# A fused Mamba and feed-forward kernel: the order of loads, activations and exponents inside a tile

## The reference, cut to what matters

```python
proj = einsum('bsd,ed->bse', layernorm(x), in_proj_w)     # gate | hBC | dt
hBC = silu(causal_conv(hBC, conv_w, 4 taps) + conv_b)     # hs | B | C
dt = clip(softplus(dt + dt_bias), 0, 100)
L = exp(segsum(dt * A))                                   # decays within a chunk of 128
Y = diagonal part (C B^T * L) @ (hs*dt) + carried part + hs*D
g = Y * silu(gate);  g = rmsnorm over each group(g) * norm_w
x = x + g @ out_proj_w.T
x = x + ffn(layernorm(x))                                 # 512 -> 1792 -> 512, quantised activations
```

## Time and profile before

| | us |
|---|---|
| median of 3 runs | 1877.3 (1875.56 to 1877.73) |
| the profiled execution, its own time | 1877.94 |
| span of the profiled execution | 1876.1 |
| TensorE busy | 1750.3 (93%) |
| VectorE busy | 1263.9 (67%) |
| GpSimd busy | 1184.9 (63%) |
| ScalarE busy | 840.9 (45%) |
| mean granted TensorE clock | 0.992 of full speed |

### The profile page before, as it was taken

The page is one execution under the profiler, slowest core; times in us unless marked ns, Lnnn a source line. Parts: engine busy times, 40 slices in busy tenths (PEclk is TensorE's granted clock), DMA queues, the critical chain, the costliest instruction groups (busy, mean ns, idle before and its releaser), DMA issues. The chain is left out here.

```text
span 1876.1 us, 34372 instructions
## 1 busy us (share of the span) xinstructions
PE 1750.3 (93%) x10392; PEld 1407.7 (75%) x10392; DVE 1263.9 (67%) x1892; ACT 840.9 (45%) x1273; POOL 1184.9 (63%) x873
## 2 busy tenths in 40 slices
PE   6899999999999999999999989999999998999998
PEld 5677787778777877787778777787778776788886
DVE  7777647772787287736874677557854774977776
ACT  4555345543564355535653555345634553322221
POOL 3487658865777568846775588558765777632430
PEclk9899999999999999999999999999999998999999
DMA  2322102210222022202230222012210221111101
GB/s 95 92 64 85 41 29 80 85 46 22 68 80 68 0 79 85 74 0 73 69 94 3 57 80 84 19 51 67 81 40 29 80 75 42 46 57 34 45 23 45
DMA packets 71341, 107.23 MB, mean 57 GB/s; under 512 B 16740, under 2 KB 25060, under 8 KB 71304
## 3 DMA queue, kind: packets, MB, share of 16 engines
q1 hardware_dynamic: 70296, 105.38, 18.8%
q10 hardware_dynamic: 1008, 1.38, 0.2%
HBM read 103.51 MB, written 3.15 MB: 57 GB/s over the span
## 5 line engine op out<-in xcount | busy, mean ns | idle before, releaser
L794 PE MATMUL proj<-xhi,w_hi 128*128 128x512 f32 x1080 | 447.2, 414 | 80.8 <-DVE gate L1116 76.9
L796 PE MATMUL proj<-xhi,w_lo 128*128 128x512 f32 x1080 | 423.7, 392 | 0.0
L795 PE MATMUL proj<-xlo,w_hi 128*128 128x512 f32 x1080 | 423.6, 392 | 0.0
L794 PEld LDWEIGHTS proj<-xhi,w_hi 128*128 128x128 f32 x1080 | 203.1, 188 | 174.7 <-DVE gate L1116 101.7
L1097 DVE SCALAR_TENSOR_TENSOR v<-proj,par_sb,v 128x510 f32<-128x510 f32 x378 | 279.9, 742 | 72.5 <-ACT v L590 51.7
L492 POOL TENSOR_TENSOR g_lo<-gated,g_hi 128x512 fp32r<-128x512 f32 x128 | 164.0, 1284 | 198.4 <-ACT g_hi L723 198.3
L427 POOL TENSOR_TENSOR w_lo<-w_raw,w_hi 128x512 fp32r<-128x512 f32 x144 | 182.5, 1286 | 138.0 <-ACT w_hi L568 138.0
L796 PEld LDWEIGHTS proj<-xhi,w_lo 128*128 128x128 f32 x1080 | 203.3, 188 | 45.0
L795 PEld LDWEIGHTS proj<-xlo,w_hi 128*128 128x128 f32 x1080 | 203.8, 189 | 35.7
L467 POOL TENSOR_TENSOR gated<-hs,gate 128x512 f32 (+1 forms) x128 | 190.0, 1506 | 51.0 <-DVE hs L1222 51.0
L590 ACT ACTIVATE v<-proj,par_sb 128x512 f32<-128x512 f32 x126 | 97.8, 776 | 248.4 <-PE proj L796 248.4
(11 more groups left out here) (164 smaller groups left out, 3360.4 us busy)
## 6 DMA issues: line engine op xcount, KB each, us to landing
w_raw<-in_win SPq DMA_DIRECT2D x144, 256.0 KB, 4.2
fade_l<-faded SPq DMA_DIRECT2D x128, 256.0 KB, 3.7
wo_raw<-in_wout SPq DMA_DIRECT2D x64, 256.0 KB, 2.6
M<-in_w SPq DMA_DIRECT2D x14, 512.0 KB, 3.8
row_r<-rows SPq DMA_DIRECT2D x256, 3.0 KB
row_l<-rows SPq DMA_DIRECT2D x256, 3.0 KB
cb<-in_w SPq DMA_DIRECT2D x7, 512.0 KB, 3.3
out<-resid SPq DMA_DIRECT2D x8, 256.0 KB, 2.0
```

The costliest lines, as they stand in the source:

```text
L794: e.matmul(o, hi_l, hi_r, start=first, stop=False)
L795: e.matmul(o, hi_l, lo_r, start=False, stop=False)
L796: return e.matmul(o, lo_l, hi_r, start=False, stop=last)
```

## The change

Four reorderings, with no instruction added or removed. SyncE issues the weight pair first in a step, ahead of wo_raw, rows and fade. ScalarE scales wo_raw between the weight casts and the second tap, casts it to wo_hi behind that tap, and does the gate's first tanh ahead of the first exponential. TensorE does the next tile's exponents ahead of y. VectorE does the gate's first silu ahead of the first weighing (so both weighings now stand between the gate's two silus), and hs's first silu behind the second step of the second convolution, no longer behind the first.

```diff
--- before.py
+++ after.py
@@ -333,6 +333,8 @@
             load_rows(0, 0)
 
             def step(g, j, par_, nxt, nxt2, ahead):
+                if nxt2:
+                    load_pair(9 * g + j + 3, split.at(g, j, 0))
                 sp.wait_ge(wolo.sem, wolo.at(g, j, 0))
                 sp.dma_start(wo_raw[:, :], wout[TPG * g + j, :, :]).then_inc(woraw.sem, 16)
                 if nxt:
@@ -340,8 +342,6 @@
                     load_rows(TPG * g + j + 1, 1 - par_)
                     sp.wait_ge(pdone.sem, pdone.at(g, j, 1))
                     load_fade(TPG * g + j + 1)
-                if nxt2:
-                    load_pair(9 * g + j + 3, split.at(g, j, 0))
 
             def window(g, nxt):
                 if nxt:
@@ -680,28 +680,29 @@
                 if nxt2:
                     act.wait_ge(ready.sem, ready.at(g, j, 0))
                     upper_pair(par_, 9 * g + j + 3)
-                if nxt:
-                    tap3(1, w, ready.at(g, j, 2), silu.at(g, j, 0))
-                    act.wait_ge(gdone.sem, gdone.at(g, j, 0))
-                    hs_tanh(hs[:, 1 - par_, :], 0, taken.at(g, j, 1))
                 act.wait_ge(woraw.sem, woraw.at(g, j, 16))
                 act.wait_ge(gused.sem, gused.at(g, 0, 0))
                 e.activation(wo_raw[:, :], wo_raw[:, :], ACT.Copy,
                              scale=par_sb[:, bass.ds(TPG * g + j, 1), K + 2:K + 3].rearrange("p a b -> p (a b)"))\
                     .then_inc(woscaled.sem, 1)
+                if nxt:
+                    tap3(1, w, ready.at(g, j, 2), silu.at(g, j, 0))
                 act.wait_ge(woscaled.sem, woscaled.at(g, j, 1))
                 e.copy(wo_hi[:, bass.ds(j, 1), :].rearrange("p a f -> p (a f)"), wo_raw[:, :])\
                     .then_inc(wohi.sem, 1)
+                if nxt:
+                    act.wait_ge(gdone.sem, gdone.at(g, j, 0))
+                    hs_tanh(hs[:, 1 - par_, :], 0, taken.at(g, j, 1))
                 if ahead:
                     bounded(g, j + 1, 0)
                 if nxt:
                     hs_tanh(hs[:, 1 - par_, :], 1, taken.at(g, j, 2))
                 if ahead:
                     bounded(g, j + 1, 1)
-                    exponential(g, j + 1, 0)
                 if nxt:
                     gate_tanh(gate[:, 1 - par_, :], 0, ready.at(g, j, 3))
                 if ahead:
+                    exponential(g, j + 1, 0)
                     exponential(g, j + 1, 1)
                 if nxt:
                     gate_tanh(gate[:, 1 - par_, :], 1, ready.at(g, j, 4))
@@ -939,9 +940,9 @@
                 turn()
                 if nxt:
                     unit(1)
-                y()
                 if ahead:
                     exponents(g, j + 1, 1 - par_)
+                y()
                 if nxt:
                     unit(2)
                     unit(3)
@@ -1087,7 +1088,7 @@
             e.tensor_scalar(par_sb[:, :, 0:K + 1], par_sb[:, :, 0:K + 1], 0.5, None, ALU.mult).then_inc(s_halved, 1)
             e.tensor_scalar(parbc_sb[:, :, :, :], parbc_sb[:, :, :, :], 0.5, None, ALU.mult).then_inc(s_halved, 1)
 
-            def conv_rest(h, weights, ntap, nconv, between=(), banks=proj):
+            def conv_rest(h, weights, ntap, nconv, between=None, banks=proj):
 
                 dve.wait_ge(tap.sem, ntap)
                 dst, src = per_batch(v[:, h, :]), per_batch(banks[h][:, :])
@@ -1097,8 +1098,8 @@
                     e.scalar_tensor_tensor(dst[:, :, d:S], src[:, :, 0:S - d], weights(K - 1 - d),
                                            dst[:, :, d:S], ALU.mult, ALU.add)\
                         .then_inc(taken.sem if d == K - 1 else convs.sem, 1)
-                    if d <= len(between):
-                        between[d - 1]()
+                    if d == 2 and between:
+                        between()
 
             def tile_weights(t):
                 return lambda k: par_sb[:, bass.ds(t, 1), k:k + 1].rearrange("p a b -> p (a b)")
@@ -1214,7 +1215,7 @@
                 if nxt:
                     conv_rest(0, w, tap.at(g, j, 1), convs.at(g, j, 0))
                     conv_rest(1, w, tap.at(g, j, 2), convs.at(g, j, 2),
-                              (lambda: hs_silu(hs[:, 1 - par_, :], 0, tanh.at(g, j, 1)),))
+                              lambda: hs_silu(hs[:, 1 - par_, :], 0, tanh.at(g, j, 1)))
                 own = tile_weights(t)
                 for h in range(2):
 
@@ -1223,11 +1224,9 @@
                                            ALU.mult, ALU.add).then_inc(ysum.sem, 1)
                 if nxt:
                     hs_silu(hs[:, 1 - par_, :], 1, tanh.at(g, j, 2))
+                    gate_silu(gate[:, 1 - par_, :], 0, tanh.at(g, j, 3))
                 if ahead:
                     weigh_own(g, j + 1, 0)
-                if nxt:
-                    gate_silu(gate[:, 1 - par_, :], 0, tanh.at(g, j, 3))
-                if ahead:
                     weigh_own(g, j + 1, 1)
                 if nxt:
                     gate_silu(gate[:, 1 - par_, :], 1, tanh.at(g, j, 4))
```

## The result

The changed kernel takes 1774.0 us (median of 4 runs, 1773.8 to 1775.0) against 1876.7 for the kernel before in the same comparison: a ratio of 0.9454, 95% interval 0.9438 to 0.9470. The profiled execution's own time is 1775.0, its span 1773.2 us.

A forecast was written before the change was run, and what follows sets the result against it. TensorE, floor 15.11 us a tile, waited for the gate's silu behind a late load. Steady tiles 82.7, first tiles 6.4 and last tiles 4.5 make 93.6 us off 1877.9: 1784 us, range 1768 to 1817.

The forecast's parts named there:

- rival A: TensorE alone sets the tile: hs's first silu stays at or under 0.97 us, interval 15.11, 1768 us; chance 0.18.
- TensorE's floor of 15.11: Shortest tile TensorE allows, 15.11 us, read from a first tile; a steady tile of 17.16 loses 2.05.
- the head of the chain: SyncE's late w_raw load: casts stood 3.21 us for it, delaying tap 1, convolution 1 and finally the gate's silu.
- Rival C: The load doesn't hold the tap; only the weighing's 1.13 us goes: interval 16.03, 1822 us; chance 0.07 with other partial gains.
- Part 1: SyncE's weight load first and ScalarE's new order: casts wait for nothing, VectorE's 1.09 us idle ahead of convolution 1 goes.
- U + 6.75: Start of ScalarE's tap 1, 6.75 us after U, the start of a tile's first projection unit; 8.6 in a steady tile before.
- rival D: Slower: exponents, now ahead of y on TensorE, wait for row loads queued behind the weights; 1972 us; chance 0.04.
- Part 2: VectorE's reordered chain from one tile's first projection unit to the next: 14.14 + s, giving an interval of 15.4 us.
- 14.14: Sum in us of all terms of VectorE's tile chain except hs's first silu.
- s: Time hs's first silu adds to VectorE's chain: taken as 1.26 us, between 0.61 and 1.84 depending on GpSimd.
- Rival B: hs's first silu meets a GpSimd piece at its start: 1.84 us, interval 15.98, 1816 us if every tile; chance 0.20.
- Part 3: TensorE's exponents ahead of y, priced at nothing; ScalarE's earlier gate tanh, without which 0.25 us a tile would be lost.

The follow-up runs named there:

- load_first_alone: The kernel before, with only SyncE's weight-pair load moved to the front of its step: 1809.4 us, ratio 0.9651.
- weigh_first: The changed kernel, with the first weighing back ahead of the gate's first silu and the first exponential ahead of its first tanh: 1822.1 us, ratio 0.9715.
- gate_tanh_behind_exp: The changed kernel, with only ScalarE's first exponential back ahead of the gate's first tanh: 1785.1 us, ratio 0.9515.
- load_last: The changed kernel, with the weight loads back at the end of SyncE's step: 1903.6 us, ratio 1.0155.
- gate_first_alone: The kernel before, with only the gate's first tanh and silu moved ahead of the first exponential and weighing: 1875.7 us, ratio 1.0005.

## Why the prediction was right, and where it was not

- **The number.** 1784 us was forecast and 1774.0 measured: right in direction, with a gain a tenth larger than forecast (102.9 for 93.6), but just below the forecast's own band (1776 to 1795, chance 0.50), in the one given to rival A (chance 0.18).
- **What bounds the kernel** was right in what it could be worth (TensorE's floor of 15.11, shown to 0.01 in 31 of 47 intervals) and incomplete in why. I called the late load "the head of the chain" and then summed a chain in which load and weighing each hold their own share. It was a loop of 17.37 us, and the sum of the changed kernel came out only because the change cuts the loop altogether.
- **Rival C** priced the gate alone at 1.13 us a tile, 53 us. It measured 0 (1.0005). The step that failed is "17.16 - 1.13": the weighing had a microsecond of cover from the load.
- **Part 1**: the loads land in time, the casts of no steady tile wait for them, tap 1 at U + 6.75. Right. That the loads move past rows, wo_raw and fade free of charge was right as well; rival D never showed.
- **Part 2** had two terms of the wrong size. The **14.14 was 0.2 too long**: in the tile that ends in a wait the chain without s is 15.53 - 1.61 = 13.92 (1.61 is the silu's 1.69 less 0.08 of overlap). Of this, 0.16 is convolution 1, 2.17 for 2.33: the prediction added 0.15 for a pause that the silu "filled and now doesn't", but behind the second step it fills that step's pause as it had filled the first's. Another 0.08 is the overlap of the two convolutions, which the sum left out. load_first_alone's 15.87 for an expected 15.85 was in part luck, as convolution 1 without the silu took 2.37 there.
- **s is no one number.** I took 1.26; over the 47 steady tiles it averages 0.95, from 0.60 to 1.65, and it costs nothing up to 15.11 - 13.92 = 1.19 (rival A's limit of 0.97 plus the 0.2 above). Only one silu in each group is longer (1.5 to 1.65), 8 of 47, and each costs its wait and the restart of the tile behind. 13.92 + 1.26 would have given 15.18, next to the measured 15.20, by luck and not by what happens. The steady tiles gave 92.0, not 82.7; this is the 9 us between 93.6 forecast and 102.9 measured. Group 0's first tile gave 1.9 for 0.8, the prologue took 1.0 that the sum doesn't have, the other terms were within 0.2.
- **Rival B's mechanism** is what makes those 8: the silu meets a fresh wo_lo, s = 1.61 in the tile above. That a long tile sets GpSimd back against VectorE fits the rows, since the next silu is shorter each time; no run tests it. **Rival A's sum** has the last tiles at 14.85 us, below the 15.11 that the same rival takes for TensorE's floor; with 15.11 it comes to 1770 us.
- **The gate's second silu** behind both weighings delayed nothing: the 15 waits for L1117 all stand ahead of a unit 0 (one in the prologue, seven in steady tiles, seven at the windows; the last group's, of 0.10 us, isn't in the list).
- **Part 3**: exponents at no price, right (1773.7). The tanh's order was priced at 0.25 us a tile; the chain grew by 0.28, and so did the mean interval (15.48 - 15.20). The second agreement is luck: 20 tiles end in a wait in place of 8, and the others show nothing of it.
- What the prediction listed under "right": the gate's waits to under 20 us (3.9), hs's first silus of 0.7 to 1.8 us (0.68 to 1.73 in steady tiles), intervals of 15.1 to 15.6 (15.10 to 15.57). All were found.

**The rule on the shared port.** By the Trainium skill (SBUF — State Buffer, "Who interferes with whom") the two engines exclude each other for whole instructions. The runs agree: a silu of 0.69 us alone ended 0.54 to 0.56 us after GpSimd's running instruction ended, whether it had waited 0.6, 1.0 or 1.8 us for it.

## What to carry to other kernels

A wait names who came last, not who sets the pace. Before pricing a move, add up every closed loop from one issue to the next of the same instruction, through the in-order queue that issues the loads as well: SyncE's 527.5 us of waiting for GpSimd looked harmless and was the loop. In a tile of fixed length, the place where an instruction meets the other engine matters as much as how long it is: one step of position was worth 27 us in the changed kernel, and by the rows of weigh_first and load_first_alone the same step costs 0.3 us a tile where the weighing comes first; taking 2 us of work from the neighbour got rid of the question. Where an engine is near its floor, price each tile by the larger of floor and chain, and don't put one mean into the chain.

## What the hardware showed that I had not expected

- A GpSimd instruction queued directly behind another does not keep the port from a waiting VectorE instruction: at 482.17 the split's second piece ended, the silu that had waited 1.03 us went first, and wo_lo took 1.74 us instead of 1.29. So a silu waits for at most the one instruction that runs when it arrives. The thirteen traces together bear this out: of the silus of hs that began with at least 0.16 us left of a GpSimd instruction, all but one of 1291 ended 0.54 to 0.56 us after that instruction. The one exception began 0.01 us after wo_lo and went first, in 0.69 us, and wo_lo took 1.85.
- The phase between the engines is stable: all groups but the last repeat 15.53, 15.24 and 15.11 at the same tiles to 0.04 us.
- A wait of TensorE costs more than its length: the tile behind it takes 15.24 us instead of 15.11 with no idle time in it, in the changed kernel and, with short silus, in gate_tanh_behind_exp.
- The loop in the kernel before answers to an edit that only looks like a reordering on ScalarE: in load_last the scaling of wo (0.72 us) stands inside it, ahead of tap 1, and the interval is 17.55 against gate_first_alone's 17.09. That difference, 0.46, is smaller than 0.72; what the rest is wasn't tried.
